# Narrowing the filler matmul of a differential-attention loop from 512 to 448 columns

## The chip, the cores and the metric

The kernel runs on all eight cores of one Trainium2 chip, one program per core, with no exchange between them. The metric is the device time of the slowest core, in microseconds (us).

## The reference, cut to what matters

Input x is 4 sequences of 4096 tokens with 1024 features. The layer adds two branches to x, both fed by a layer norm without weights:

```python
xn = layernorm(x)
q = (xn @ Wq.T), k = (xn @ Wk.T)      # 32 half heads of 32 features
v = (xn @ Wv.T)                       # 16 heads of 64 features
aw = softmax(q k^T)                   # one map for each half head
aw = aw[half 0] - lam * aw[half 1]    # differential attention
attn = rmsnorm(aw @ v) * g * (1 - LAMBDA_INIT) @ Wo.T
h = silu(xn @ w1 * s1) * (xn @ w2 * s2)
h = gelu(h @ h1 * s); h = gelu(h @ h2 * s)
out = x + attn + (h @ w3 * s)
```

The matmul that this change touches computes nothing of this: its result is never read.

## The kernel before, in words

Each core owns 2048 query tokens of one sequence and sees all 4096 key tokens. The parts follow one another in time:

1. Layer norm of 32 row tiles, transposed on TensorE into `xn_own` and `xn_oth` (bf16).
2. Attention, for 8 groups `g` of two heads. A group first projects k, v and q (L391), transposes v (L419) and takes maxima of squares for the exponent's bias (L464 to L506). Then for each head `p` of the two, one loop of 130 steps (`gkt`) runs over 4 query blocks `qv` of 512 queries, and in each over 32 key tiles `kt` of 128 keys. A step computes the scores of key tile `gkt` and the product with v of the tile two steps earlier.
3. The output projection of attention (L709), 32 units of 8 matmuls.
4. The feed-forward part in two chunks of 1024 tokens (L844, L857, L911, L984, L1020), which has no filler matmul.

Every engine works off its queue in order, and the queues' order is the order in which `prog.do` is called. Waits are semaphore values. The steps of the loop, in the names that the prediction uses:

- **filler**: `emit_warm` (L516), an identity times columns of `xn_own` into `pwarm`, the second bank of `psS`. It is issued once ahead of the scores, and once ahead of the product with v, and once ahead of each of the 32 units of the output projection. It waits on semaphores that are long passed.
- **scores**: two matmuls with 32 rows each (L558), for the two half heads, into `psA` or `psB` in turn. They wait for the exponential that last read that buffer.
- **exponential**: one ScalarE instruction of 128x1024 (L572) from `psA` or `psB` into one of three buffers `e`.
- **product with v**: two matmuls (L532, L536) that accumulate over 32 key tiles into the two banks of `psO`, 65 rows out, the last of them the softmax sum.

When a query block's last key tile is summed (this happens in step `kt` = 1 of the next block), VectorE copies `psO` out (L592, L596) and the first product with v of the next block waits for that. Then VectorE works out a scale (L606 to L615), and six pieces of the block's end are issued from a list, `pending`, at `kt` = 8 (L620, a matmul that waits for L615), 10 (L630 to L635), 16 (L640), 18 (L646 to L665, with a logarithm and an exponential on ScalarE, L653 and L657), 24 (L670) and 26 (L681). There are 8 x 2 x 4 = 64 query blocks, so 2048 steps with scores.

The loop, without the lambdas' bodies:

```python
for gkt in range(130):
    if gkt < 128:
        qv, kt = divmod(gkt, 32)
        if kt in (8, 10, 16, 18, 24, 26) and pending:
            pending.pop(0)()
        emit_warm()
        ...
    if gkt < 2:
        continue
    ...
    emit_warm()
    emit_av(tk, t_ % 3)
```

Of the kernel before, what the change touches and what calls it, by code (L numbers as in the profile page):

```python
# [110 lines left out]
def build(tap=()):  # L111
# [33 lines left out]
    identb = A("identb", [128, 128], BF16).ap()  # L145
# [16 lines left out]
    xn_own = A("xn_own", [128, 8 * OWN], BF16).ap()  # L162
# [98 lines left out]
    if True:  # L261
# [21 lines left out]
        pwarm = psS[:, 512:1024]  # L283
# [52 lines left out]
        if True:  # L336
# [27 lines left out]
            for g in range(NG):  # L364
# [149 lines left out]

                def emit_warm():
                    prog.do("tensor", lambda e: e.matmul(  # L516
                        pwarm, identb, xn_own[:, 0:512],
                        start=True, stop=True),
                        waits=[(sv, marks.get("stat_v", 0)), (sa, m_xn_a),
                               (sg, m_init)])  # L520

                for p in range(2):
# [19 lines left out]
                    for gkt in range(130):  # L542
                        if gkt < 128:
# [4 lines left out]
                            kp3 = gkt % 3  # L548
                            Sps = S01[kp]
                            emit_warm()  # L550
                            for e_i in range(2):
                                w0 = []
# [27 lines left out]
                        t_ = gkt - 2  # L580
                        tqv, tk = divmod(t_, 32)
                        emit_warm()
                        emit_av(tk, t_ % 3)
                        if tk != 31:
# [110 lines left out]
            for u, (qc, ot) in enumerate((qc, ot) for qc in range(4)  # L695
                                         for ot in range(8)):
                    emit_warm()
                    if u == 4:
                        while len(pending) > 2:
# [414 lines left out]
```

How the kernel before makes its waits and increments, by code:

```python
            def body(eng):  # L71
                for ws, fn, incs in self.q[name]:
                    for s, v in ws:
                        eng.wait_ge(s.h, v)
                    if fn is None:
                        if incs:
                            ins = eng.nop()
                            for s, k in incs:
                                ins.then_inc(s.h, k)
                        continue
                    ins = fn(eng)
                    for s, k in incs:
                        ins.then_inc(s.h, k)
```

## Time and profile before

| what | value |
|---|---|
| time, median of 2 runs | 6814.92 us (6776.85 to 6852.99) |
| time of the profiled execution | 6564.84 us |
| its span on the slowest core (core 3) | 6563.3 us |
| spans of the eight cores | 6551.6 to 6563.3 us |
| mean granted TensorE clock, all cores | 0.948 to 0.950 |
| TensorE matmuls busy | 5942.5 us, 91% of the span |
| ScalarE busy | 2792.3 us, 43% |
| VectorE busy | 1531.3 us, 23% |

The profiled execution is one run under the hardware profiler. It took 6564.84 us where the two timed runs took 6776.85 and 6852.99 us, so its durations are used for differences and the median of the timed runs for the level. In the trace a matmul's busy time overlaps that of the next one, so the cost of a matmul in a stream is read from one start to the next, and not from its duration. PEclk is the clock that TensorE was granted, as a share of 2.4 GHz: 1.00 is 2.4 GHz and 0.50 is 1.2 GHz.

### The profile page before, as it was taken

Reading aid. Unit: us, or ns where it says so; the run is one execution under the profiler, and the core shown is the slowest. Engines: PE = TensorE matmul, PEld = TensorE weight load, DVE = VectorE, ACT = ScalarE, POOL = GpSimd, SP = SyncE. Lnnn points to the kernel's source line nnn. Section 1 sums busy time; section 2 is a strip of 40 time slices with the busy share of each in tenths; the row PEclk is TensorE's granted clock in tenths of the full one; section 3 lists DMA queues with packets and bytes.
Section 4 is the critical chain, followed back from the end, with each engine's and each line's share of the span. In section 5 each row is a group of like instructions: output and inputs, shape, how many; then the busy total and the mean of one; then the engine's idle time right before and its main releaser. Section 6 shows DMA issues by size and latency. Waiting matters only on the chain.

```text
span 6563.3 us, 71702 instructions; the slowest of 8 cores (6551.6 to 6563.3 us)
## 1 busy us (share of the span) xinstructions
PE 5942.5 (91%) x26176; PEld 2277.4 (35%) x26176; DVE 1531.3 (23%) x2062; ACT 2792.3 (43%) x2888; POOL 170.0 (3%) x325
## 2 busy tenths in 40 slices
PE   2599899899898998998998989999999899999997
PEld 1233233233232232332332334444444344444443
DVE  7523333332323323333233332100000110000001
ACT  3377477476575784774875751100000011000000
POOL 0000000000000000000000001000000010000000
PEclk9899899899898998998998999999999899999998
DMA  2100000000000000000000004434444344443343
GB/s 84 33 1 1 7 1 4 4 1 7 1 1 7 1 1 7 1 1 13 1 1 1 1 26 89 84 76 77 77 77 77 87 97 87 77 76 73 76 88 89
DMA packets 76596, 247.95 MB, mean 38 GB/s; under 512 B 8608, under 2 KB 25056, under 8 KB 57824
## 3 DMA queue, kind: packets, MB, share of 16 engines
q0 software_dynamic: 44000, 193.03, 16.2%
q1 hardware_dynamic: 32256, 50.35, 2.3%
q8 instruction: 219, 3.59, 0.2%
q14 instruction: 121, 0.99, 0.0%
HBM read 419.50 MB, written 16.78 MB: 66 GB/s over the span
## 4 chain that ended last, share of the span: by engine, by line
PE 77%; DVE 15%; ACT 4%; issue 3%; DVEq 0%; DMA 0%; ACTq 0%; SPq 0%
PE pM L911 27%; PE psS L516 13%; PE psO L532 5%; PE psO L536 5%; PE psA L391 4%; PE psA L558 4%; PE psB L558 4%; PE pM L984 4%; PE pM L844 3%; PE pM L857 3%; DVE rows L615 3%; DVE rows L606 3%; ACT e L572 2%; DVE smll L479 2%; PE psA L709 1%
## 5 line engine op out<-in xcount | busy, mean ns | idle before, releaser
L911 PE MATMUL pM<-a,hbT 128*128 128x512 bf16 x8192 | 1770.1, 379 | 8.9 <-DVE a L876 6.1
L516 PE MATMUL psS<-xn_own,identb 128*128 128x512 bf16 x4128 | 1635.1, 396 | 0.0
L572 ACT ACTIVATE e<-psA,bias_gp 128x1024 bf16<-128x1024 f32 x1024 | 1140.9, 1114 | 366.9 <-PE psA L558 343.2
L572 ACT ACTIVATE e<-psB,bias_gp 128x1024 bf16<-128x1024 f32 x1024 | 1141.1, 1114 | 269.9 <-PE psB L558 245.1
L911 PEld LDWEIGHTS pM<-a,hbT 128*128 128x128 bf16 x8192 | 801.6, 98 | 977.4 <-issue 12.6
L532 PE MATMUL psO<-e,vgt 128*65 128x512 bf16 x2048 | 801.7, 391 | 45.9 <-DVE o1s L596 45.8
L536 PE MATMUL psO<-e,vgt 128*65 128x512 bf16 x2048 | 798.9, 390 | 0.0
L516 PEld LDWEIGHTS psS<-xn_own,identb 128*128 128x128 bf16 x4128 | 405.3, 98 | 740.6 <-issue 554.5
L1009 DVE TENSOR_TENSOR f3s<-f3s,asld 128x1024 f32<-128x1024 f32 x16 | 19.6, 1225 | 2041.7 <-ACT f3s L1003 2041.7
L558 PE MATMUL psA<-qg,kg 32*128 32x512 bf16 x2048 | 407.1, 394 | 42.6 <-ACT e L572 42.6
L924 ACT ACTIVATE a<-pM,h2ss 128x1024 bf16<-128x1024 f32 x64 | 71.3, 1114 | 815.9 <-PE pM L911 815.9
L558 PE MATMUL psB<-qg,kg 32*128 32x512 bf16 x2048 | 409.3, 397 | 0.0
L924 ACT ACTIVATE a<-pM,h1ss 128x1024 bf16<-128x1024 f32 x64 | 71.3, 1114 | 784.8 <-PE pM L911 784.8
L536 PEld LDWEIGHTS psO<-e,vgt 128*65 128x65 bf16 x2048 | 235.2, 115 | 220.7 <-issue 24.4
L532 PEld LDWEIGHTS psO<-e,vgt 128*65 128x65 bf16 x2048 | 252.3, 123 | 65.3 <-issue 63.4
L558 PEld LDWEIGHTS psA<-qg,kg 32*128 32x128 bf16 x2048 | 98.3, 91 | 452.2 <-issue 452.2
L558 PEld LDWEIGHTS psB<-qg,kg 32*128 32x128 bf16 x2048 | 96.3, 91 | 454.8 <-issue 454.8
L984 PE MATMUL pM<-a,hbT 128*128 128x512 bf16 x1024 | 251.6, 412 | 2.8 <-ACT a L924 2.8
L844 PE MATMUL pM<-xn_own,w12b 128*128 128x512 bf16 x1024 | 232.8, 380 | 0.9 <-DVE wqb L726 0.9
L592 DVE COPY o0s<-psO 65x512 f32<-65x512 f32 x64 | 44.0, 687 | 803.9 <-PE psO L536 803.9
L857 PE MATMUL pM<-xn_own,w12b 128*128 128x512 bf16 x1024 | 231.5, 379 | 0.0
L870 ACT ACTIVATE t0b<-pM,s1s 128x1024 f32<-128x1024 f32 x64 | 71.3, 1114 | 356.7 <-PE pM L857 356.7
(122 smaller groups left out, 3221.0 us busy)
## 6 DMA issues: line engine op xcount, KB each, us to landing
hbT<-h POOLq DMA_DIRECT2D x128, 1024.0 KB, 8.5
w12b<-w POOLq DMA_DIRECT2D x128, 256.0 KB, 4.3
ph0x<-x SPq DMA_DIRECT2D x32, 512.0 KB, 3.3
hbT<-w POOLq DMA_DIRECT2D x16, 1024.0 KB, 8.5
xldp<-x SPq DMA_DIRECT2D x128, 64.0 KB, 2.1
asld<-attn_scr SPq DMA_DIRECT2D x16, 512.0 KB, 4.0
out<-outT SPq DMA_DIRECT2D x16, 512.0 KB, 2.9
attn_scr<-wosb SPq DMA_DIRECT2D x16, 256.0 KB, 2.4
```

Of the source, the lines that this page charges most:

```text
L391: src=src, toff=toff: e.matmul(pj, wb[:, 128 * ic:128 * (ic + 1)], src[:, OWN * ic + toff:OWN * ic + toff + 512], start=(ic == 0), stop=(i ...
L516: prog.do("tensor", lambda e: e.matmul(pwarm, identb, xn_own[:, 0:512], start=True, stop=True), waits=[(sv, marks.get("stat_v", 0)), (sa, ...
L532: e.matmul(po0, vsl, e01[eb][:, 0:512], start=(kt == 0), stop=(kt == 31)),
L536: e.matmul(po1, vsl, e01[eb][:, 512:1024], start=(kt == 0), stop=(kt == 31)),
L558: kt=kt, p=p, qv=qv, tp=tp: e.matmul(Sps[:, 512 * e_i:512 * (e_i + 1)], kg[64 * p + 32 * e_i: 64 * p + 32 * (e_i + 1), 128 * kt:128 * (kt ...
L572: e.activation(e01[kp3], Sps, AF.Exp, bias=bias_gp[:, p:p + 1]),
L606: prog.do("vector", lambda e: e.reciprocal(rows[:, 512:1024], o1s[64:65, :]))
L615: prog.do("vector", lambda e: e.reciprocal(rows[:, 0:512], o0s[64:65, :]))
L844: ic=ic, hc=hc, coff=coff: e.matmul(pa[:, 512 * hc:512 * (hc + 1)], w[:, 128 * ic:128 * (ic + 1)], xn_own[:, OWN * ic + coff + 512 * hc: O ...
L857: ic=ic, hc=hc, coff=coff: e.matmul(pb2[:, 512 * hc:512 * (hc + 1)], w[:, 128 * ic:128 * (ic + 1)], xn_own[:, OWN * ic + coff + 512 * hc: ...
L911: ic=ic, hc=hc, srcap=srcap: e.matmul(pp[:, 512 * hc:512 * (hc + 1)], w[:, 128 * ic:128 * (ic + 1)], srcap[:, TCH * ic + 512 * hc: TCH * i ...
L984: hc=hc: e.matmul(pp[:, 512 * hc:512 * (hc + 1)], w[:, 128 * ic:128 * (ic + 1)], a1[:, TCH * ic + 512 * hc: TCH * ic + 512 * (hc + 1)], st ...
```

## The change

The filler matmul reads 448 columns in place of 512, and writes 448. Its weights (the 128x128 identity), its waits, its place in the queue and the number of times that it is issued stay as they are, and no other instruction changes or moves.

```diff
 def emit_warm():
     prog.do("tensor", lambda e: e.matmul(
-        pwarm, identb, xn_own[:, 0:512],
+        pwarm[:, 0:448], identb, xn_own[:, 0:448],
         start=True, stop=True),
         waits=[(sv, marks.get("stat_v", 0)), (sa, m_xn_a),
                (sg, m_init)])
```

## Rows read from the trace of the kernel before

**Rows 1.** The page's chain that ended last, by engine and by line

```profile
PE 77%; DVE 15%; ACT 4%; issue 3%; DVEq 0%; DMA 0%; ACTq 0%; SPq 0%
PE pM L911 27%; PE psS L516 13%; PE psO L532 5%; PE psO L536 5%; PE psA L391 4%; PE psA L558 4%; PE psB L558 4%; PE pM L984 4%; PE pM L844 3%; PE pM L857 3%; DVE rows L615 3%; DVE rows L606 3%; ACT e L572 2%; DVE smll L479 2%; PE psA L709 1%
```

**Rows 2.** The page's groups: the filler

```profile
L516 PE MATMUL psS<-xn_own,identb 128*128 128x512 bf16 x4128 | 1635.1, 396 | 0.0
```

**Rows 3.** Timeline of PE, one step of the loop: start us, us, what

```profile
2178.10 0.39 PE L516 MATMUL psS<-xn_own,identb 128*128 128x512 bf16 x1
2178.33 0.38 PE L532 MATMUL psO<-e,vgt 128*65 128x512 bf16 x1
2178.54 0.38 PE L536 MATMUL psO<-e,vgt 128*65 128x512 bf16 x1
2178.76 0.38 PE L516 MATMUL psS<-xn_own,identb 128*128 128x512 bf16 x1
2179.07 0.39 PE L558 MATMUL psA<-qg,kg 32*128 32x512 bf16 x2
2179.39 0.39 PE L516 MATMUL psS<-xn_own,identb 128*128 128x512 bf16 x1
```

**Rows 4.** Timeline of ACT around one end piece (L653, L657)

```profile
2164.32 1.11 ACT L572 ACTIVATE e<-psB,bias_gp 128x1024 bf16<-128x1024 f32 x1 [0.18 <-PE psB L558]
2165.52 0.72 ACT L653 ACTIVATE rows<-rows,epsb 1x512 f32<-1x512 f32 x1
2166.34 0.63 ACT L657 ACTIVATE rows<-rows 1x512 f32<-1x512 f32 x1
2167.06 1.11 ACT L572 ACTIVATE e<-psA,bias_gp 128x1024 bf16<-128x1024 f32 x1
...
2171.88 1.11 ACT L572 ACTIVATE e<-psA,bias_gp 128x1024 bf16<-128x1024 f32 x1
2173.09 1.11 ACT L572 ACTIVATE e<-psB,bias_gp 128x1024 bf16<-128x1024 f32 x1
2174.46 1.11 ACT L572 ACTIVATE e<-psA,bias_gp 128x1024 bf16<-128x1024 f32 x1 [0.25 <-PE psA L558]
```

**Rows 5.** Waits of PE between 311 and 3990 us: total, times, longest

```profile
PE psS L620 <- DVE rows L615: 92.4, 56, 2.1
PE psO L532 <- DVE o1s L596: 45.8, 48, 1.3
PE psA L558 <- ACT e L572: 42.6, 71, 0.9
```

**Rows 6.** Timeline of DVE, then of PE, from a block's end to L620

```profile
1506.67 0.69 DVE L592 COPY o0s<-psO 65x512 f32<-65x512 f32 x1 [12.33 <-PE psO L536]
1513.57 3.34 DVE L615 RECIPROCAL rows<-o0s 1x512 f32<-1x512 f32 x1
...
1514.95 0.38 PE L536 MATMUL psO<-e,vgt 128*65 128x512 bf16 x1
1517.06 0.37 PE L620 MATMUL psS<-rowsb,ones64f 1*64 1x512 bf16 x1 [1.73 <-DVE rows L615]
```

**Rows 7.** Stretches: us, busy (x) of PE, PEld, DVE, ACT, POOL, PEclk, DMA, GB/s

```profile
1514.20:1517.60 3.40, 1.68 (x8) 0.51 (x7) 2.71 (x1) 1.47 (x2) 0.00 (x0) 1.00 0.00 0
1517.60:1521.00 3.40, 3.40 (x11) 0.87 (x11) 2.05 (x3) 1.11 (x1) 0.00 (x0) 0.50 0.00 0
...
1506.70:1555.90 49.20, 45.93 (x198) 14.55 (x197) 14.82 (x16) 37.02 (x35) 0.00 (x0) 0.93 0.00 0
...
2186.80:2232.90 46.10, 42.82 (x196) 14.10 (x195) 14.81 (x15) 37.00 (x35) 0.00 (x0) 1.00 0.00 1
2232.90:2280.60 47.70, 44.43 (x196) 14.34 (x195) 14.80 (x15) 37.01 (x35) 0.00 (x0) 0.96 0.00 1
...
2109.70:2115.00 5.30, 2.33 (x5) 0.34 (x5) 3.97 (x6) 0.00 (x0) 0.00 (x0) 0.50 0.00 0
2140.00:2145.00 5.00, 5.00 (x15) 1.17 (x14) 0.00 (x0) 3.36 (x4) 0.00 (x0) 0.50 0.00 0
...
311.20:3888.50 3577.30, 3241.50 (x14012) 1070.23 (x14012) 1150.85 (x1526) 2452.98 (x2328) 14.88 (x28) 0.93 0.02 3
```

**Rows 8.** Timeline of PE at the low clock: one step between two fillers

```profile
2142.40 0.61 PE L516 MATMUL psS<-xn_own,identb 128*128 128x512 bf16 x1
2144.76 0.61 PE L516 MATMUL psS<-xn_own,identb 128*128 128x512 bf16 x1
```

## Prediction

> **What bounds the kernel now.** I read the chain of waits on the page first, then the filler's group, then the timeline of TensorE in the loop, then the waits of TensorE, and last the granted clock by stretches.
>
> The chain [rows 1] says that TensorE sets 77% of the span, and that the filler alone (L516) holds 13%. The filler is issued 4128 times [rows 2]: twice in each of 2048 steps and once ahead of each of 32 units of the output projection. So it isn't idle time being filled: somewhere it stands on the path.
>
> The timeline of one step [rows 3] shows where. The starts are 2178.10 (filler), 2178.33 (L532), 2178.54 (L536), 2178.76 (filler), 2179.07 (scores), 2179.39 (the next filler). The step takes 1.29 us with no idle mark on any row. A matmul of 512 columns holds the next one off by 0.21 to 0.23 us. Ahead of the scores it is 0.31 us, as they also pay for a weight load. ScalarE's exponential waits 0.18 us for the scores each time in the steady steps, and where it is late it runs with 1.21 us from start to start (2171.88 to 2173.09) [rows 4]. So the steady step is bound by TensorE at 1.29 us, and ScalarE follows 0.08 us behind it.
>
> Three waits break this pattern [rows 5]. L620 waits for VectorE's reciprocal L615 56 times, 92.4 us in all. L532 waits for VectorE's copy L596 48 times, 45.8 us. The scores wait for the exponential 71 times, 42.6 us; that is mostly once per query block, behind the logarithm and exponential of the block's end piece (L653, L657) [rows 4]. The first two belong to one chain of VectorE: it starts with the block's last product with v (L592 at 1506.67) and ends where L620 may start (1517.06) [rows 6]. That is 10.4 us, and TensorE stands still at its end for 1.73 us. In those 10.4 us VectorE sets the time, whatever TensorE does.
>
> The clock is the last view. A query block takes 46.1 us where the clock is 1.00 throughout, 47.7 us where its mean is 0.96, and 49.2 us where it is 0.93 [rows 7]. The rows around 1517 show how it falls: TensorE worked half of 3.4 us because of the stop before L620, and the next 3.4 us have the clock at 0.50. So one such stretch costs about 1.6 us of a block. Over the whole loop the mean is 0.93 [rows 7], so 2 x 0.07 x 3577 = 500 us passed at 1.2 GHz. The long low stretches around the start of a group, which the rows at 2109.7 and 2140.0 us belong to, take nearly 50 us in each of seven groups, some 340 us. About 160 us are left, or 47 short stretches of 3.4 us.
>
> **The change part by part.** It removes 64 of 512 columns from 4128 matmuls and moves nothing.
>
> One filler: the nearest rows are the start-to-start times of 512 columns, 0.216 us, so 64 columns are 0.216 x 64/512 = 0.027 us. Two in a step make 0.054; I take 0.053. The bounds: nothing, if a matmul has a floor that doesn't shrink with its columns, and 0.027 us each at the full clock (twice that at 1.2 GHz). I take the upper end, because at 1.2 GHz the same step takes 2.36 us [rows 8] against 1.29: TensorE's part goes with its clock and therefore with columns. The Trainium skill says otherwise on the page "TensorE: Matmul & The Clock Gate", section "Back-to-back issue gap": in a real stream with weight loads 131 ns per matmul at 512 columns and 81 ns at 128. An estimate from that page would be (131 - 81) x 64/384 = 8 ns per filler, and the whole sum below would shrink to about 25 us. The trace disagrees with its 131 ns: it has 216 ns in exactly such a stream.
>
> The new step is 1.29 - 0.053 = 1.237 us. ScalarE's floor is 1.21 us [rows 4], so it doesn't become the bound, but only 0.03 us is left.
>
> One query block, in its pieces:
> - From L592 to L620, 10.4 us: nothing is gained. Some ten fillers stand between the wait for the copy and L620; their 0.27 us are added to the stop, which goes from 1.73 to about 2.0 us.
> - From L620 to the next L592, 35.7 us (46.1 - 10.4): 26 steps from kt = 8 to kt = 1 of the next block. Each would give 0.053 us. But behind L653 and L657 the scores wait for ScalarE, and the time from the scores ahead of these two to the released ones is set by ScalarE: 3 steps that give nothing. So 23 x 0.053 = 1.22 us.
>
> 63 blocks have such a second piece ahead of another block's end: 63 x 1.22 = 77 us. The first block has 34 steps with no end piece before it: 1.8 us. The first 8 steps of the seven later groups have no stop in them: 7 x 8 x 0.053 = 3.0 us. The output projection has 32 fillers: 32 x 0.027 = 0.9 us, or nothing where it waits for VectorE. The feed-forward part has none. The sum is 82 us at an unchanged number of low-clock stretches.
>
> The unknown term is that number. Its bounds from rows: if none of the 47 is left, 47 x 1.55 = 73 us more are gained, 155 in all. If each of the 48 long stops (those with L532's wait) brings two, 96 stretches, 49 x 1.55 = 76 us are lost again, and 6 are left. For more of them speaks that the stop grows by a seventh and that TensorE does less in each step. For fewer speaks only that stops of the same length sometimes bring one and sometimes none (the blocks at 2186.8 and 2232.9) [rows 7], so that the spacing of the stops matters too, and it changes from 47.7 to 46.5 us. I take the nearest row, the present number, so zero, and keep half of each end for the range: 44 to 118 us saved.
>
> Against the profiled execution's own 6564.84 us the sum gives 6483. The timed runs are 3.8% longer, and no row says where; 82 us would become 85 if it were spread evenly. I put the 82 us on the median: 6815 - 82 = 6733 us, 1.2% less. A measurement of this kernel can tell about 2% from no change, which is 136 us.
>
> **The rivals.**
>
> *Fewer falls of the clock.* The stops fall out of step with whatever makes the clock drop. Saved are 118 to 155 us, 6660 us at the end. For it: the uneven pattern at equal stops. Against it: each stop is longer than before. 0.13.
>
> *More falls, still a gain.* Saved are 6 to 44 us, about 6790 us. For it: the longer stops, and stretches that already come in pairs (the block of 49.2 us). 0.14.
>
> *The low clock holds: slower.* After a fall TensorE must show enough work to be given 2.4 GHz back, and the fillers are what provides it; with an eighth fewer filler columns the steps at 1.2 GHz may no longer do. A step then takes 2.36 - 0.107 = 2.25 us in place of 1.24, 1.0 us more; over the 26 steps of a block 26 us. Three such blocks eat the 82 us; at one block in four (16) the time is 6815 - 82 + 416 = 7149 us. For it: full work at 2140 us still ran at 0.50 for 5 us [rows 7], so regaining isn't immediate. Against it: in the blocks read here the clock came back after one or two short stretches each time, and the filler is only one part of a step in which TensorE is never idle. 0.04.
>
> *Nothing gained.* The columns saved are waited away: ScalarE binds, or a matmul has a floor as by the page above. Time 6815 us, or 6790 by that page's figures. For it: ScalarE is only 0.03 us away. Against it: in rows 4 ScalarE waits for TensorE outside the few steps behind L657. 0.07.
>
> **How the numbers follow.** The forecast, an unchanged number of falls within half of the ends, has 0.62. The low end is the faster timed run less 110 us, 6667; the high end the slower timed run less 44 us, 6809; since both extremes seldom meet I take 6670 to 6803. That takes in most of the second rival and part of the first. Faster by over 2% needs 136 us, which only the top of the first rival or a lucky level of the runs gives: 0.08. Slower by over 2% is the third rival: 0.04. The rest is 0.88.
>
> **What would show it.** Right: in a steady step the fillers' starts are 1.237 us apart, with L532 0.20 us behind the filler and the scores 0.28; the time from L592 to L620 stays 10.4 us while L620's wait grows to about 2.0 us each, some 105 us in all; the scores' wait for the exponential grows by about 0.16 us per block; a block without a low stretch takes 44.9 us. The loop's mean clock stays at 0.93 and its span falls from 3577 to about 3495 us. Wrong: steps that stay above 1.25 us, an exponential without a wait for the scores in steady steps, or low stretches longer than 7 us within a block.

## The result and the profile after

The changed kernel takes 6599.13 us (median of 42 runs, 6503.38 to 6986.57) against 6648.75 us before (41 runs). The ratio is 0.9928, with a 95% interval of 0.9907 to 0.9948: 0.7% faster, where 1.2% was forecast. That is a small gain, but the interval is clear of 1. In some executions of any of these kernels the cores of a die are granted a lower clock than usual, and the two timed runs of before that the forecast took its level from (6776.85 and 6852.99 us) were such; the ratio leaves them out, before takes 6562 to 6565 us without them, and where the profile of an experiment has such a die, the cores of the other are quoted.

The spans of the cores in the profiled executions show the same gain. Before they were 6551.6 to 6563.3 us, mean 6559.2; after, mean 6496.7:

```profile
core: us from the first to the last instruction, mean granted TensorE clock
core 0: 6493.3 us, clock 0.945
...
core 2: 6508.2 us, clock 0.943
core 3: 6496.0 us, clock 0.944
```

So the mean gain is 62.5 us against a forecast of 82, and the mean clock fell from 0.949 to 0.944. The share that is missing sits in that clock. The rows of these two profiles know two levels, 1.00 and 0.50, so the time at 1.2 GHz is 2 x (1 - clock) x span, about 670 us before and 725 us after.

The timeline of two steady steps on PE of the changed kernel, which answers to [rows 3] (start us, us, what):

```profile
2419.76 0.36 PE L516 MATMUL psS<-xn_own,identb 128*128 128x448 bf16 x1
2419.96 0.38 PE L532 MATMUL psO<-e,vgt 128*65 128x512 bf16 x1
2420.17 0.38 PE L536 MATMUL psO<-e,vgt 128*65 128x512 bf16 x1
2420.39 0.35 PE L516 MATMUL psS<-xn_own,identb 128*128 128x448 bf16 x1
2420.67 0.39 PE L558 MATMUL psB<-qg,kg 32*128 32x512 bf16 x2
2420.99 0.36 PE L516 MATMUL psS<-xn_own,identb 128*128 128x448 bf16 x1
2421.19 0.38 PE L532 MATMUL psO<-e,vgt 128*65 128x512 bf16 x1
...
2422.23 0.36 PE L516 MATMUL psS<-xn_own,identb 128*128 128x448 bf16 x1
```

The filler holds L532 off by 0.20 us in place of 0.23, and the scores by 0.28 in place of 0.31. From 2419.76 to 2420.99 and on to 2422.23 a step is 1.23 and 1.24 us; it was 1.29. The whole length of the 64 columns is saved, twice.

The waits of PE in the loop, which answer to [rows 5] (total us, times, longest), and the stop before L620, which answers to [rows 6]:

```profile
PE psS L620 <- DVE rows L615: 107.8, 56, 2.4
PE psA L558 <- ACT e L572: 53.1, 71, 1.0
PE psO L532 <- DVE o1s L596: 48.4, 48, 1.3
```

```profile
1318.52 0.38 PE L536 MATMUL psO<-e,vgt 128*65 128x512 bf16 x1
1320.88 0.37 PE L620 MATMUL psS<-rowsb,ones64f 1*64 1x512 bf16 x1 [1.99 <-DVE rows L615]
```

All three waits grew. L620's went from 92.4 to 107.8 us, one stop from 1.73 to 1.99 us; L532's, which lies in the same chain of VectorE, from 45.8 to 48.4 us. The scores' wait went from 42.6 to 53.1 us in 71 times, 0.15 us each.

Stretches of one query block each, and then the loop, of core 2 after the change. They answer to [rows 7] (us, busy of PE, PEld, DVE, ACT, POOL, then PEclk):

```profile
1310.50:1355.40 44.90, 41.15 (x198) 14.14 (x197) 14.83 (x16) 37.00 (x35) 0.00 (x0) 1.00 0.00 1
1264.00:1310.50 46.50, 42.75 (x198) 14.43 (x197) 14.82 (x16) 37.01 (x35) 0.00 (x0) 0.96 0.00 1
1714.00:1762.00 48.00, 44.25 (x198) 14.64 (x197) 14.85 (x16) 37.02 (x35) 0.00 (x0) 0.93 0.00 1
355.00:3822.00 3467.00, 3102.95 (x13754) 1055.10 (x13754) 1148.26 (x1523) 2401.28 (x2284) 15.10 (x28) 0.92 0.02 3
```

A block is 1.2 us shorter at each clock (46.1, 47.7 and 49.2 us before). But the loop's mean clock is 0.92 where it was 0.93.

The spans can be taken apart by the starts of L592, L620 and L844, and the granted clock summed over each piece (us, means of the eight cores):

| piece | before | after | forecast of the difference |
|---|---|---|---|
| up to the first filler | 307.9 | 307.0 | 0 |
| the first block | 46.0 | 45.0 | -1.8 |
| L592 to L620 (56 times) | 583.3 | 583.3 | 0 |
| the same across the start of a group (7 times) | 644.3 | 637.8 | -3.0 |
| L620 to the next L592 (63 times) | 2303.2 | 2249.6 | -77 |
| of that at 1.2 GHz | 157.0 | 207.6 | 0 |
| last block's end and output projection | 76.9 | 75.8 | -0.9 |
| feed-forward | 2597.6 | 2598.1 | 0 |

The 50.6 us more at 1.2 GHz are 14.8 stretches of 3.41 us; at the 1.55 us that one costs, 23 us. And -77 + 23 = -54, where -53.6 was measured.

Low stretches can follow one another without a break. Call such a run of them a fall. Counted in the traces of all eight cores, behind the 448 stops before L620 (384 long ones, and 64 short ones, at the block end that falls between the two heads of a group):

| kernel | long stops: us, falls | short stops: us, falls | falls of one, two, three stretches |
|---|---|---|---|
| before | 1.73 (32 of them 2.1), 299 | 1.02, 0 | 230, 69, 0 |
| after | 1.99 (32 of them 2.3 to 2.4), 282 | 1.34, 42 | 187, 109, 28 |

So the long stops, though longer, did not bring more falls. What was added are the falls behind the short stops, and second and third stretches.

### The profile page after: what moved, and what is told of

The parts are those of the page before. It is cut to its first block, busy times and chain, and to the rows that moved or that the text cites. A ratio compares the mean times of both kernels' runs of the same rounds, so it can differ in the third digit from the quotient of the medians.

```text
span 6508.2 us, 71702 instructions; the slowest of 8 cores (6493.2 to 6508.2 us)
## 1 busy us (share of the span) xinstructions
PE 5860.0 (90%) x26176; PEld 2281.5 (35%) x26176; DVE 1531.4 (24%) x2062; ACT 2790.2 (43%) x2888; POOL 170.5 (3%) x325
## 4 chain that ended last, share of the span: by engine, by line
PE 75%; DVE 15%; ACT 5%; issue 3%; DVEq 0%; ACTq 0%; DMA 0%
PE pM L911 27%; PE psS L516 12%; PE psO L532 5%; PE psO L536 5%; PE psA L391 4%; PE psA L558 4%; PE pM L984 4%; PE psB L558 4%; ACT e L572 3%; PE pM L844 3%; PE pM L857 3%; DVE rows L615 3%; DVE rows L606 3%; DVE smll L479 2%; PE psA L709 1%
## 5 line engine op out<-in xcount | busy, mean ns | idle before, releaser
L516 PE MATMUL psS<-xn_own,identb 128*128 128x448 bf16 x4128 | 1533.0, 371 | 0.0
L532 PE MATMUL psO<-e,vgt 128*65 128x512 bf16 x2048 | 808.0, 395 | 48.8 <-DVE o1s L596 48.5
L558 PE MATMUL psA<-qg,kg 32*128 32x512 bf16 x2048 | 412.3, 399 | 53.2 <-ACT e L572 53.1
L532 PEld LDWEIGHTS psO<-e,vgt 128*65 128x65 bf16 x2048 | 253.3, 124 | 67.5 <-issue 65.6
L844 PE MATMUL pM<-xn_own,w12b 128*128 128x512 bf16 x1024 | 232.8, 380 | 0.9 <-DVE wqb L726 0.9
L592 DVE COPY o0s<-psO 65x512 f32<-65x512 f32 x64 | 44.0, 687 | 771.2 <-PE psO L536 746.9
```

Source lines behind the costliest of these rows:

```text
L516: prog.do("tensor", lambda e: e.matmul(pwarm[:, 0:448], identb, xn_own[:, 0:448], start=True, stop=True), waits=[(sv, marks.get("stat_v", ...
L532: e.matmul(po0, vsl, e01[eb][:, 0:512], start=(kt == 0), stop=(kt == 31)),
L558: kt=kt, p=p, qv=qv, tp=tp: e.matmul(Sps[:, 512 * e_i:512 * (e_i + 1)], kg[64 * p + 32 * e_i: 64 * p + 32 * (e_i + 1), 128 * kt:128 * (kt ...
L844: ic=ic, hc=hc, coff=coff: e.matmul(pa[:, 512 * hc:512 * (hc + 1)], w[:, 128 * ic:128 * (ic + 1)], xn_own[:, OWN * ic + coff + 512 * hc: O ...
```

## The experiments

The theory after this result: the columns are saved in full, and the additional low-clock stretches take 23 us back. What remained was why there are more of them. Theory S: the stop before L620 is longer (1.99 in place of 1.73 us), and a longer stop drops the clock more often or for longer. Theory R: the steps behind the stop hold less work for TensorE, so the clock comes back later.

**Narrow fillers only ahead of the stop** (e1_narrow_ahead).

```diff
-emit_warm()              # 512 columns, both places in a step
+emit_warm(448 if 2 <= gkt % 32 <= 7 else 512)
```

> 448 columns only in steps kt = 2 to 7, ahead of the stop before L620; 512 everywhere else. Nothing is gained in these steps, since VectorE's chain of 10.39 us sets them; the stop grows from 1.73 to about 2.0 us as in the changed kernel. After the change the low clock took 208 us of the pieces from L620 to the next L592 (mean of the cores), against 157 before. Theory S (the longer stop causes the additional falls): about 200 us here, and the span 6559 + 22 = about 6580 us. Theory R (thinner steps regain the clock later): 157 us here and about 6559 us, since every step after a fall has 512 columns.

Measured: ratio to before 1.0043 (1.0025 to 1.006), so slower by 0.4%. The spans had a mean of 6574.7 us, 15.5 more than before, and 200.8 us were spent at 1.2 GHz between L620 and L592. That is what theory S expected, 43.8 us more where the whole change has 50.6: 343 of the 384 long stops brought a fall (299 before), 6 of the 64 short ones, and 102 falls had a second stretch (69 before). The steps ahead of the stop also hold less work here; no run has the longer stop without that. The cores differ:

```profile
core 0: 6592.5 us, clock 0.941
core 1: 6575.5 us, clock 0.945
core 2: 6560.8 us, clock 0.948
...
core 5: 6594.5 us, clock 0.941
```

Core 2 has the clock and the time of before, and core 5 has 258 us at 1.2 GHz between L620 and L592. The program is the same on all, so the stop's length alone doesn't decide whether the clock falls. Where the stop lies in time is the likely other part: before the change, with the same two lengths, the first stop of a group brought a fall 34 times in 64 and the second 63 times. No run takes this by itself.

**Narrow fillers everywhere else** (e2_narrow_after).

```diff
-emit_warm()              # 512 columns
+emit_warm(512 if 2 <= gkt % 32 <= 7 else 448)
```

> The mirror: 448 columns everywhere but in steps kt = 2 to 7, so the stop stays at 1.73 us and the steps behind it are the thin ones. Both theories: 77 us less in the pieces from L620 to L592 at equal clock. Theory S: 157 us at the low clock as before, span about 6475 us. Theory R: about 208 us at the low clock, span about 6497 us as in the changed kernel. A third, the spacing of the stops (46.5 in place of 47.7 us): some other number, with falls that are fewer but come in pairs or the reverse.

Measured: spans with a mean of 6482.3 us, 14 less than with the whole change, 2232.7 us between L620 and L592 and 169.3 us of it at 1.2 GHz. So 12 us at the low clock are left that the stop's length does not explain, 5.6 us of time: R or the changed spacing, which this run doesn't part. The 12 us are a balance of larger parts: fewer long stops brought a fall (263 of 384), but 26 of the 64 short ones did, at 1.05 us, and 107 of all falls had a second stretch (69 before). The sum holds: -77 + 12.3/3.41 x 1.55 = -71.4, measured -70.5. The two partial changes add 44 and 12 us of low clock, the whole change 51. They don't simply add up, and short stops of 1.05 us fell more often here than those of 1.31 us in the run before (26 and 6 of 64), so length alone doesn't explain the falls.

**The stop taken away, 512 columns** (e3_late_512).

```diff
-if kt in (8, 10, 16, 18, 24, 26) and pending:
+if kt in (10, 12, 16, 18, 24, 26) and pending:
```

> 512 columns as before, but the end pieces are issued at kt = 10, 12, 16, 18, 24, 26, so L620 comes two steps (2.58 us) later than its 10.39 us chain needs. If the stop before L620 is what drops the clock within a block: L620's wait (92 us) is gone, the short low stretches (157 us) too, worth 157/3.41 x 1.55 = 71 us, and the span is 6560 - 92 - 71 = about 6400 us. Rival (the stop of 0.94 us before L532 or the start of a block is enough): L620's wait gone but the low stretches stay, about 6468 us.

Measured on cores 0 to 3, mean 6391.4 us, where about 6400 were expected:

```profile
core 0: 6390.0 us, clock 0.960
core 1: 6392.5 us, clock 0.960
core 2: 6386.7 us, clock 0.961
core 3: 6396.5 us, clock 0.959
```

Core 3's waits of PE no longer have a row for L620, and the two others are unchanged to the tenth:

```profile
PE psS L464 <- DVE smll L482: 58.6, 126, 0.8
PE psO L532 <- DVE o1s L596: 45.8, 48, 1.3
PE psA L558 <- ACT e L572: 42.6, 71, 0.9
```

Between L620 and L592 not a single stretch was at 1.2 GHz, on any core. So the stop before L620 is what dropped the clock within blocks, and the shorter one before L532, which is still there, doesn't here. Moving two pieces of the block's end by two steps is worth about 168 us, more than twice what the change's columns are.

**The same with 448 columns** (e4_late_448).

```diff
-if kt in (8, 10, 16, 18, 24, 26) and pending:
+if kt in (10, 12, 16, 18, 24, 26) and pending:
-pwarm, identb, xn_own[:, 0:512],
+pwarm[:, 0:448], identb, xn_own[:, 0:448],
```

> The same with 448 columns. Without the stop the steps ahead of L620 count too: about 28 of 32 steps give 0.053 us, 64 x 28 x 0.053 = 95 us below the 512-column version with late pieces, so about 6305 us if no falls are left. Rival (the low clock holds or ScalarE's 1.21 us becomes the bound with only 0.03 us to spare): 60 us or less below it, steps above 1.24 us.

```profile
core 0: 6297.6 us, clock 0.958
...
core 3: 6298.1 us, clock 0.958
core 4: 6291.8 us, clock 0.959
...
core 7: 6300.8 us, clock 0.958
```

Measured: ratio 0.9603 (0.9581 to 0.9625), and mean span 6297.6 us, 94 us below cores 0 to 3 with 512 columns, where 95 were expected. Without the stop, the steps ahead of L620 count too, and the same change of columns gives 94 us in place of 62.5.

**384 columns with the stop** (e5_384).

```diff
-pwarm, identb, xn_own[:, 0:512],
+pwarm[:, 0:384], identb, xn_own[:, 0:384],
```

> 384 columns, end pieces at kt = 8 as in the changed kernel. ScalarE floors the step at 1.207 us instead of 1.29 - 2 x 0.0533 = 1.183, so a step gives 0.083 us, not 0.107; the stop before L620 grows to 1.73 + 10 x 0.0533 = about 2.2 us. Theory (a linear gain less low stretches that a longer stop brings): 63 x 23 x 0.083 = 120 us less than before, less about 50 us for yet more low stretches, span about 6490 us. Rival (the low clock holds with thinner steps): low stretches of tens of us within blocks, mean clock below 0.90, span above 6600 us.

Measured on cores 0 to 3: 6452.4 to 6456.5 us, some 105 us less than before, and 255 to 262 us at 1.2 GHz between L620 and L592. L620's wait:

```profile
PE psS L620 <- DVE rows L615: 122.2, 56, 2.6
PE psA L558 <- ACT e L572: 65.6, 72, 1.2
```

The direction holds: narrower still, a longer stop, another 50 us of low clock, and still a gain. The rival (the low clock holds) did not appear. The expected 6490 us was 36 too high. A block without low clock takes 43.8 us against 46.1, 0.4 us less than expected, or 25 us in all: the exponentials' intervals around L640 and L670 shrank too, from 1.70 to 1.42 us and from 1.37 to 1.21. The other 11 us came from the first block, the group starts and the output projection, which the expectation left out.

**384 columns without the stop** (e6_late_384, and once more as e10_late_384_again). The edit is that of the run before and the later end pieces together:

```diff
-if kt in (8, 10, 16, 18, 24, 26) and pending:
+if kt in (10, 12, 16, 18, 24, 26) and pending:
```

> 384 columns with late end pieces, so without the stop. If ScalarE's 1.207 us is the floor, a step goes from 1.237 to 1.207: 0.03 us x 27 steps x 64 = 52 us less than 448 columns with late pieces (6298 us mean of the cores), so about 6250 us. Rival (clock): low stretches at the start of groups grow longer than 48 us each, or appear within blocks.

> The 384-column version with late pieces once more, for an interval: profiled spans were 6211 to 6221 us against 6552 to 6563 before, a ratio of 0.948. The same again is expected, 0.945 to 0.952.

Measured: 6211.2 to 6221.3 us, 81 us below 448 columns, where 52 were expected. The second time the ratio to before was 0.9466 (0.9419 to 0.9512), as expected. ScalarE now runs through in the steady steps, with 1.21 us from start to start and no idle mark. L620 on PE (here at 1229.73, core 1) breaks this once:

```profile
1226.99 1.11 ACT L572 ACTIVATE e<-psB,bias_gp 128x1024 bf16<-128x1024 f32 x1
1228.19 1.11 ACT L572 ACTIVATE e<-psA,bias_gp 128x1024 bf16<-128x1024 f32 x1
1229.40 1.11 ACT L572 ACTIVATE e<-psB,bias_gp 128x1024 bf16<-128x1024 f32 x1
1230.88 1.11 ACT L572 ACTIVATE e<-psA,bias_gp 128x1024 bf16<-128x1024 f32 x1 [0.36 <-PE psA L558]
1232.08 1.11 ACT L572 ACTIVATE e<-psB,bias_gp 128x1024 bf16<-128x1024 f32 x1
```

The same place with 448 columns and late end pieces (e4_late_448, core 1):

```profile
1256.77 1.11 ACT L572 ACTIVATE e<-psB,bias_gp 128x1024 bf16<-128x1024 f32 x1
1258.44 1.11 ACT L572 ACTIVATE e<-psA,bias_gp 128x1024 bf16<-128x1024 f32 x1 [0.56 <-PE psA L558]
```

So the interval around L620 is 1.48 us in place of 1.67. A block without low clock takes 41.45 us in place of 42.84, and the 1.39 us are found in the exponentials' intervals: 20 steps give 0.03 us each (the expectation had 27; the others were at 1.21 us already), those around L620 and L640 give 0.19 and 0.17 us, and the one around the stop before L532 gives 0.43 (1.96 in place of 2.39). TensorE's own step would be 1.29 - 4 x 0.027 = 1.18 us, an estimate from the starts. So TensorE is now a little faster than ScalarE, and part of what an end piece or a stop costs it no longer reaches ScalarE; 0.27 us of L620 still do. I had left that out of the expectation.

**256 columns without the stop** (e7_late_256). Late end pieces again, and

```diff
-pwarm, identb, xn_own[:, 0:512],
+pwarm[:, 0:256], identb, xn_own[:, 0:256],
```

> 256 columns with late end pieces. ScalarE is the floor already at 384, so nothing more is gained at the full clock: about 6250 us. Rival (the filler's work is what wins the full clock back at the start of each group and holds it): with half the filler the low clock lasts; a step at 1.2 GHz is 2.36 - 4 x 0.107 = 1.93 us, 0.7 us above ScalarE's floor, up to 2048 x 0.7 = 1450 us more.

```profile
core 2: 6251.6 us, clock 0.940
...
core 4: 6192.2 us, clock 0.954
...
core 7: 6254.6 us, clock 0.940
```

Measured: 6192 to 6255 us, mean 6223.3, so the same as 384 within the scatter of the cores, which now differ by 1%. Between L620 and L592 they spent 37 to 198 us at 1.2 GHz, where 384 columns had none: with so little filler the clock falls in spite of late pieces. A block without low clock takes 40.8 us in place of 41.45, so something more was gained at the full clock, against the expectation, and the low clock took it back. Core 7's waits show that L620 waits again, though only 0.5 us each, and that the wait for the exponential is twice that of 448 columns (53.3 us on this core):

```profile
PE psA L558 <- ACT e L572: 108.6, 82, 1.9
...
PE psO L532 <- DVE o1s L596: 50.4, 48, 1.4
...
PE psS L620 <- DVE rows L615: 21.8, 46, 0.8
```

The falls don't begin at L620. Of 166 that begin within blocks on the eight cores, 156 begin behind the scores' wait for the exponential, the one behind L653 and L657 (147 times one of 1.6 us), and 10 behind the stop before L532 (1.4 us). The first of core 7, in PE's timeline and in stretches as in [rows 7]:

```profile
375.95 0.39 PE L558 MATMUL psA<-qg,kg 32*128 32x512 bf16 x2 [1.59 <-ACT e L572]
...
376.60:380.00 3.40, 3.40 (x12) 0.98 (x11) 0.00 (x0) 2.64 (x3) 0.00 (x0) 0.50 0.02 5
380.00:393.60 13.60, 13.60 (x43) 4.08 (x41) 0.68 (x1) 7.80 (x7) 0.00 (x0) 0.50 0.00 0
```

This wait was 0.9 us at most with 512 columns. So thinner fillers made a new stop that drops the clock, and 34 of the falls behind it lasted 17 us. The ratio to before was 0.9504 (0.9424 to 0.9584).

**No filler in the loop** (e9_late_none). The filler's result is never read, so nothing of the computation is left out. The end pieces are the late ones, and the output projection keeps its fillers, with 448 columns.

```diff
-emit_warm()              # both places in a step
```

> No filler in the loop, only in the output projection, with late end pieces; the filler computes nothing, so the output is the same. TensorE's step would be 1.29 - 2 x 0.22 = 0.85 us at the full clock and about 1.5 us at 1.2 GHz. If the clock regains 2.4 GHz without the filler: ScalarE's floor, 1.207 us, about 6250 us. If the filler is what keeps it: all 2048 steps at 1.5 us, 2048 x 0.3 = 600 us more, about 6850 us, with a mean clock near 0.5 in the loop.

```profile
core 0: 6882.4 us, clock 0.724
...
core 4: 6865.6 us, clock 0.727
```

Measured: ratio 1.0478 (1.0398 to 1.0559), mean clock 0.725, near the 6850 us that was expected if the filler is what keeps the clock. The feed-forward part has no filler; the loop alone was at 0.54 in its first 3089 us:

```profile
311.00:3400.00 3089.00, 2877.92 (x7899) 619.91 (x7924) 923.90 (x1243) 1936.44 (x1846) 15.04 (x28) 0.54 0.02 3
```

So the forecast's rival of a lasting low clock is real; it lies between 256 and no columns, and 448 is well away from it.

**The stop taken away by a shorter chain** (e11_early_mark_448). L620 reads `rowsb` and not what L615 writes. Its mark is taken one instruction earlier, the end pieces stay at kt = 8, and the filler has 448 columns.

```diff
+marks["c1"] = sv.n
 prog.do("vector", lambda e: e.reciprocal(
     rows[:, 0:512], o0s[64:65, :]))
-marks["c1"] = sv.n
```

> 448 columns, end pieces at kt = 8 as in the changed kernel, but L620 no longer waits for the second reciprocal L615, whose result it doesn't read: the chain from L592 to it is 10.39 - 3.45 = 6.9 us, and TensorE gets to L620 only after 10.39 - 2.0 = 8.4 us. If that chain alone makes the stop, and the stop the falls, this is the version with late pieces over again by another way: L620's wait 0, no low stretch within blocks, about 6300 us. Rival (what helped there was the later place of the other pieces): a stop or low stretches stay, nearer to 6497 us.

Measured: in five of the six timed runs the four cores of one die had spans of 6292.1 to 6301.9 us, mean 6296.7. In the profiled execution all eight cores have 740 to 1017 us at a granted clock of 0.81 and took 6395.0 to 6476.7 us; but on no core was any of the time between L620 and L592 at 1.2 GHz, and L620 has no row among the waits of PE (core 3). That agrees with the 6297.6 us of late pieces with 448 columns. Two different edits that share only the missing stop have the same effect, so it is the stop, and not where the other pieces stand.

## Why the prediction was right or wrong

- The filler stands on the path and its columns are saved in full, 0.027 us each: right (two steps in a row of 1.23 and 1.24 us in the timeline). The estimate of 8 ns per filler from the Trainium skill's page "TensorE: Matmul & The Clock Gate", section "Back-to-back issue gap", and the 25 us that follow from it, are refuted by the starts in the timeline: 0.20 us behind a filler of 448 columns, 0.23 behind one of 512.
- L592 to L620 gives nothing, and the stop takes up the gain: right, 583.3 us before and after, and a stop of 1.99 us for "about 2.0".
- Three steps are lost behind L653 and L657: right; the scores' wait grew by 10.5 us, 0.16 us per block as forecast.
- A block without a low stretch takes 44.9 us: right.
- The first block and the group starts: -1.0 and -6.5 us for -1.8 and -3.0. The starts gained a little more; their time at 1.2 GHz fell from 338.8 to 332.4 us, which I had not foreseen.
- "I take the nearest row, the present number, so zero": this is the term of the sum that failed. The number of low stretches between L620 and L592 rose from 46 to 61 (157.0 and 207.6 us over 3.41), which cost 23 us of the 82. The saving of 62.5 us is still within the forecast's own 44 to 118 us, between its 82 and the second rival's 44. I had named the longer stop as the ground for it and then set the term to zero because the spacing of the stops argued the other way. What the runs show in its place: thin fillers ahead of the stop alone bring 44 us of low clock, thin fillers behind it alone 12, both together 51. The low clock within blocks depends on the stop (it is gone when the stop is), but how often it falls and how long it lasts follows neither theory by itself: the long stops brought fewer falls (282 for 299), the short stops 42 for none, and 28 falls had a third stretch. The forecast's upper bound counted only the 48 long stops of a core, and its sign of being wrong, a low stretch of more than 7 us within a block, came true in these 28. What decides in the single case stays open.
- The level: "I put the 82 us on the median" is the step that put the time outside the range. That median was of two runs that were 3.2% and 4.4% above the 6564.84 us of the profiled execution, and 41 runs of the same kernel have 6648.75 us. The time of 6599.13 us lies outside 6670 to 6803 for that reason alone: with 6648.75 us as the level, the same 44 to 118 us give 6531 to 6605. With the profiled execution as the level, the forecast of 6483 stands against 6509.78 us, and 6447 to 6521 would have held it. The forecast saw that no row explained the 3.8%, so its range should have reached down to the profiled level. (Its low end of 6667 also took off 110 us where its own bound is 118.)
- The loop: its mean clock was to stay at 0.93 and its span to fall from 3577 to about 3495 us. It was 0.92 and 3514 us on the same core, for the same reason as the failed term.
- The third rival (the clock stays low) did not happen at 448 or 384 columns. With 256 columns the clock stayed low for 17 us at times, and without fillers for most of the loop.

## What to carry to other kernels

When an in-order engine runs toward a wait whose end another engine sets, what you save ahead of that wait only makes the stop longer; count only the steps behind it. If stops of that engine also drop its clock, as here, the longer stop costs twice, so first remove the stop (a later consumer, or a mark that leaves out work that the consumer doesn't read) and only then thin the work. A filler that keeps the clock was best here when just narrow enough to reach the next engine's floor: 384 columns reach ScalarE's 1.21 us, 256 gain nothing in sum and let the clock falter, and without fillers the kernel is 4.8% slower than before. And when timed runs and a profiled execution disagree by more than the effect, a forecast needs more runs for its level, or a range that holds both. The best version was 384 columns with late end pieces, 5.3% below the kernel before.

## What the runs showed of the hardware that I had not expected

- Stops of TensorE much shorter than the low stretch that follows can drop its clock: stops of 1.73 us (some 2.1) in an otherwise full loop brought a fall of 3.4 or 6.8 us 299 times in 384, and none of the 64 stops of 1.02 us did. There is no fixed length: 42 of 64 stops of 1.34 us brought one after the change, 6 of 64 of 1.31 us with narrow fillers only ahead of the stop, and 26 of 64 of 1.05 us with narrow fillers only behind it.
- The stop of 0.94 us before L532 brought none before the change. At 1.35 to 1.4 us it did so twice on eight cores with 448 columns and late pieces, twice with 384, and ten times with 256.
- The same program, in the same execution, falls at a different number of stops on different cores: 164 to 258 us at 1.2 GHz in the run with narrow fillers ahead of the stop, and 37 to 198 us with 256 columns.
- A TensorE that is a little faster than the engine it feeds can keep 2.4 GHz (384 columns and late pieces: no low stretch between L620 and L592 on any core), but not with much less work: in a loop without fillers the mean was 0.54.
